# First attention of a fused transformer kernel: where TensorE computes the four heads' output product, and in which PSUM bank

## What is computed

```
q, k = rope(hs @ Wq.T), rope(hs @ Wk.T);  v = hs @ Wv.T;  g = hs @ Wg.T
s  = clip(hs @ Ws1.T @ Ws2.T + bs2, -32, 32);  z = cumlogsumexp(s, over tokens)
A  = where(mask, q @ k.T * scale, 0)
ok = exp(-z) * (A @ exp(s))                       # slot scores
qv = softmax(ok)
W2 = where(mask, (qv * exp(-z)) @ exp(s).T, 0)    # slot weights
o  = W2 @ v                                       # values
o_g = rmsnorm(o) * gnorm * silu(g)
x   = x + o_g @ Wo.T                              # output product
```

## Time and profile before

| | us |
|---|---|
| median of 3 runs (lowest, highest) | 1480.73 (1479.02, 1484.91) |
| the profiled execution's own time | 1484.12 |
| its span, first to last instruction | 1482.3 |
| PE busy, of the span | 1342.1 (91%) |
| PEld busy | 1069.0 (72%) |
| DVE busy | 921.8 (62%) |
| POOL busy | 556.5 (38%) |
| ACT busy | 517.4 (35%) |
| mean granted TensorE clock, as a share of 2.4 GHz | 0.967 |

### The profile page before, as it was taken

One profiled execution on the slowest core, in us unless ns is written; L12 is line 12 of the kernel. 1 busy time (PEld: TensorE's weight loads), 2 busy tenths in 40 slices (PEclk: granted clock), 3 DMA queues, 4 the chain that ended last, 5 costly groups with the idle time before them and its releaser, 6 DMA issues. The chain is left out here.

```text
span 1482.3 us, 47081 instructions
## 1 busy us (share of the span) xinstructions
PE 1342.1 (91%) x19926; PEld 1069.0 (72%) x19926; DVE 921.8 (62%) x1825; ACT 517.4 (35%) x1188; POOL 556.5 (38%) x608
## 2 busy tenths in 40 slices
PE   2899999999999999999986699999998688997996
PEld 2678788888788788788765577777777466776665
DVE  2777777777777777777764474242423245666886
ACT  2244444444444444444343313231322122222343
POOL 0656555556565565655532212222212111112111
PEclk9999999999999999999999799999999789997999
DMA  6000000010000100000001500000000630000620
GB/s 188 5 14 13 13 13 13 14 31 13 13 13 13 31 13 13 7 3 2 2 3 38 206 12 1 0 0 0 0 1 0 184 107 0 0 0 2 197 67 22
DMA packets 33416, 47.09 MB, mean 32 GB/s; under 512 B 6974, under 2 KB 22552, under 8 KB 32728
## 3 DMA queue, kind: packets, MB, share of 16 engines
q1 hardware_dynamic: 31048, 42.20, 9.3%
q10 hardware_dynamic: 2112, 2.10, 0.5%
q0 software_dynamic: 80, 0.26, 0.1%
HBM read 42.19 MB, written 2.36 MB: 30 GB/s over the span
## 5 line engine op out<-in xcount | busy, mean ns | idle before, releaser
L419 PE MATMUL OE<-w_o,ogT_s 128*128 128x256 f32 x512 | 137.9, 392 | 0.7 <-ACT ogT_s L506 0.7
L875 POOL TENSOR_TENSOR hT_lo<-h,hT_hi 128x512 fp32r<-128x512 f32 x44 | 56.8, 1292 | 193.1 <-ACT hT_hi L1048 193.1
L233 POOL TENSOR_TENSOR turned<-t1c,t2s 128x512 f32<-128x512 f32 x62 | 78.8, 1271 | 123.0 <-DVE t2s L636 123.0
L661 DVE RECIPROCAL enz<-SC 128x128 f32<-128x128 f32 x128 | 121.3, 949 | 2.9 <-PE SC L367 2.5
L274 POOL TENSOR_TENSOR exz<-ex,enz 128x256 f32<-128x256 f32 x64 | 47.4, 740 | 181.2 <-ACT ex L572 181.2
L1111 DVE SCALAR_TENSOR_TENSOR t<-th,m 128x512 f32<-128x512 f32 (+1 forms) x56 | 38.4, 685 | 121.3 <-ACT th L1053 93.5
L318 PE MATMUL PJ<-hs_hi,w_hi 128*128 128x512 f32 x248 | 102.6, 414 | 0.0
L329 PE MATMUL PJ<-w_hi,hs_lo 128*128 128x512 f32 x256 | 100.3, 392 | 0.5 <-issue 0.5
L329 PE MATMUL PJ<-w_hi,hs_hi 128*128 128x512 f32 x256 | 100.8, 394 | 0.0
L329 PE MATMUL PJ<-w_lo,hs_hi 128*128 128x512 f32 x256 | 100.3, 392 | 0.0
L318 PE MATMUL PJ<-hs_hi,w_lo 128*128 128x512 f32 x248 | 97.3, 392 | 0.0
(11 more groups left out here) (383 smaller groups left out, 3574.9 us busy)
## 6 DMA issues: line engine op xcount, KB each, us to landing
we_ring<-in_we SPq DMA_DIRECT2D x64, 256.0 KB, 3.1
w_raw<-in_w_slices SPq DMA_DIRECT2D x48, 128.0 KB, 2.1
turned<-in_w_slices ACTq DMA_DIRECT2D x4, 512.0 KB, 7.9
xres<-in_x SPq DMA_DIRECT2D x2, 1024.0 KB, 14.4
out_rows<-xres SPq DMA_DIRECT2D x16, 128.0 KB, 1.7
w1r<-in_w1i SPq DMA_DIRECT2D x1, 1408.0 KB, 6.6
w_s<-in_w SPq DMA_DIRECT2D x2, 682.0 KB
w_o<-in_wo SPq DMA_DIRECT2D x1, 1024.0 KB, 5.4
```

Of the source, the lines that this page charges most:

```text
L233: pool.tensor_tensor(to[:, 0, :], x1c[:, :], x2s[:, :], ALU.subtract)
L419: m = pe.matmul(OE[:, SW:SW + D], ogT_s[:, i % 2, h * P:(h + 1) * P], w_o[:, i // G % 2, h, :], start=(h == 0), stop=(h == HQ - 1))
L661: dve.reciprocal(enz[:, cols], SC[:, SW:2 * SW][:, cols]).then_inc(z_rec, 1)
L875: eng.tensor_tensor(hT[1][s, m % 2, :], h[s, m % 2, :], hT[0][s, m % 2, :].bitcast(F32), ALU.subtract).then_inc(second, 1)
```

## The change

In `heads_out` the product is summed in the lower half of `PJ[0]` in place of the upper half of `OE`, and its four heads are issued one by one: before `turn_og`, between `slot_weights` and `turn_es`, between `scores` and `values`, and between `values` and `slot_scores`. Before, it was two and two, at the first two of these places. The waits follow the bank: `heads_out` waits until `PJ[0]` has been read (`x1_sin`, `v_ev`) where it waited for `ok_z`; `proj_v` waits for `y_add`, and `slot_scores` no longer does. DVE does `mask_scores(i+1)` ahead of `y_out(i-2)`.

```diff
             def proj_v(i, part):
                 if part.start == 0:
                     pe.wait_ge(x1_sin, min(FIRST + i, TURNS))
+                    pe.wait_ge(y_add, i - 2) if i >= 3 else None
                     pe.wait_ge(v_ev, i)
@@
             def slot_scores(i):
                 pe.wait_ge(a_mask, i + 1)
                 pe.wait_ge(ok_z, i)
-                pe.wait_ge(y_add, i - 2) if i >= 3 else None
@@
                     pe.wait_ge(ogT_ev, i + 1)
                     pe.wait_ge(y_add, i)
-                    pe.wait_ge(ok_z, min(i + 3, STEPS))
+                    pe.wait_ge(x1_sin, min(i + 3 + FIRST, TURNS))
+                    pe.wait_ge(v_ev, min(i + 3, STEPS))
                     pe.wait_ge(wo_scaled, i // G + 1)
                 for h in range(*part):
-                    m = pe.matmul(OE[:, SW:SW + D], ogT_s[:, i % 2, h * P:(h + 1) * P], w_o[:, i // G % 2, h, :],
+                    m = pe.matmul(PJ[0][:, 0:D], ogT_s[:, i % 2, h * P:(h + 1) * P], w_o[:, i // G % 2, h, :],
                                   start=(h == 0), stop=(h == HQ - 1))
@@
                 if now:
                     turn_p(i)
                 if i >= 2:
-                    heads_out(i - 2, (0, 2))
+                    heads_out(i - 2, (0, 1))
                 if i >= 1:
                     turn_og(i - 1)
                 if now:
                     slot_weights(i)
                 if i >= 2:
-                    heads_out(i - 2, (2, HQ))
+                    heads_out(i - 2, (1, 2))
                 if one:
                     turn_es(i + 1)
                     scores(i + 1)
+                if i >= 2:
+                    heads_out(i - 2, (2, 3))
                 if now:
                     values(i)
+                if i >= 2:
+                    heads_out(i - 2, (3, HQ))
                 if one:
                     slot_scores(i + 1)
@@
             def y_out(i):
                 dve.wait_ge(y_mm, i + 1)
-                dve.tensor_tensor(xres[:, i % G, :], OE[:, SW:SW + D], xres[:, i % G, :], ALU.add).then_inc(y_add, 1)
+                dve.tensor_tensor(xres[:, i % G, :], PJ[0][:, 0:D], xres[:, i % G, :], ALU.add).then_inc(y_add, 1)
@@
                     z(i + 1, 1)
+                if one:
+                    mask_scores(i + 1)
                 if i >= 2:
                     y_out(i - 2)
                 if one:
-                    mask_scores(i + 1)
                     slot_max(i + 1)
```

## The result

The changed kernel takes 1516.2 us (median of 4 runs, 1512.8 to 1518.1), the kernel before 1481.1 us beside it: a ratio of 1.0223, 95% interval 1.0199 to 1.0247. The forecast was 1510, 2.0% slower, with a range of 1498 to 1523. The profiled execution has a span of 1515.3 us, 33.0 more than before.

A forecast was written before the change was run, and what follows sets the result against it. TensorE, busy 649.8 of 660 us, was taken as the bound; +30.5 us for the moved heads, +6 for `turn_es`, -9 for gaps and +1.5 for last rounds gave +29 on 1480.7, so 1510 us, range 1498 to 1523.

The forecast's parts named there:

- isolated head until small tiles: One head alone between small tiles: 0.43 us, +0.10 behind small tiles, +0.09 to 0.10 until they restart, so 0.63, twice.
- `values` until a head: Edge from `values`, now 0.86 us to `slot_scores`: with a head behind it 1.01, so +0.15.
- TensorE is a plain sum: First attention's loop: a round sums TensorE's start-to-start distances; anything else counts only where it makes TensorE wait.
- Changes of tile: TensorE switching between whole-array and small-tile work loses about 0.1 us each way; moved heads cost about +0.50 us a round.
- Rival D: Not slower: a head between small tiles costs only its 0.43 us; 1472, or 1478 with the `turn_es` wait; chance 0.07.
- Rival E: Weight loads hidden: the 0.10 us a head pays behind small tiles goes, 1498 us; chance 0.05.
- The new wait of `turn_es`: Ahead of `scores`, `turn_es` comes early and its load waits for ACT's copy to `ogT_s`: +0.1 us a round, +6 us.
- Rival C: Chain ahead of `scores` bounds: `ogT_s`, then `turn_es` and `wm` 0.2 us later a round, +12, 1522 us; chance 0.10.
- The longer rounds: Gaps, mostly inside `slot_scores`, about 10 us in all, read as waits for code; most go, -9 us.
- rival B: The gaps stay, being no code waits or packets falling due elsewhere as densely: 1519 us; chance 0.14.
- DVE and the new bank at nothing: DVE's work ahead of `scores` (`wm` 0.3 us early) and the new bank with its waits cost nothing.
- The last rounds: Four or five rounds wait for POOL's norm in `turn_og`; a moved head no longer fills it: +0.3 each, +1.5 us.

The follow-up runs named there:

- f3: Changed kernel with both late heads together behind `scores` and none behind `values`: 1500.4 us, ratio 1.0131.
- f5: Changed kernel with heads one, two, one: before `turn_og`, two behind `slot_weights`, one behind `values`, none behind `scores`: 1501.1 us, ratio 1.0134.
- f7: Changed kernel with two heads before `turn_og`, none between `slot_weights` and `turn_es`, one behind `scores`, one behind `values`: 1541.0 us, ratio 1.0396.
- f1: Changed kernel (its bank, waits and VectorE order) with the heads two and two at the two old places: 1485.9 us, ratio 1.0022.

## Why the prediction was right, point by point

| term | predicted | measured |
|---|---|---|
| isolated head until small tiles | 0.63 us, twice | 0.63, 0.63 |
| `scores` until a head | 0.69 | 0.68 |
| `values` until a head | 1.01 | 1.01 |
| late `turn_es` | +0.1 | +0.12 (0.09 and 0.03) |
| regular round | 11.95 to 12.05 | 12.01 |
| gaps | -9 us | -10 us |
| first attention | +29 us | +28.5 us |
| last rounds, over the +0.6 of each | +1.5 us | +1.6 us |
| behind it | 0 | +4.5 us in this profile, +2.3 in the second |

- *TensorE is a plain sum* held: the regular round of every variant came out within 0.1 us of what was added up for it beforehand.
- *Changes of tile* held, as a price for each place (f3) and with the dearer edge behind `values` (f5). Rival D is out: the extra in a round is 0.60, far above 0.16. Rival E is out too: the load of an isolated head starts with its matmul, and the distance of 0.63 has the 0.10 in it.
- *The new wait of `turn_es`* held in size (0.12 against 0.1), and f5 and f7 show it go and grow. Two errors in its working cancel, and that is luck. It had the hand-over at 0.06, taken from DVE's `ok`; from the copy `ogT_s` to the matmul it is 0.14. The late load was put at 0.10 and showed as 0.03. The sign named for it, ScalarE's `ogT_s` in the waits, did not come: the view says "issue". Rival C, a chain ahead of `scores` that is 0.2 us later still, is out: `turn_es` pays 0.12, and `wm` is done 0.34 before `scores`.
- *The longer rounds* went, and the list's shift with the count of the gaps shows why: rival B, by which they would stay, is out. I had bounded the relief by nothing and 10 us and taken 9. What I held against B, that all gaps lie in one line, was misread: three of the 11 lie in other lines. What I held for B, that their place hangs on the position in the list, is true, but from it does not follow that they stay.
- *DVE and the new bank at nothing* held (f1).
- *The last rounds* held. Four of the last five wait for POOL's norm, and that wait grew from 0.58 to 0.60 us each to 1.02 or 1.03, as forecast. The five, from one `turn_p` to the next, take 52.03 us before (from 742.64) and 56.70 now (from 765.23), +4.67; less 0.6 for each round, 1.6 to 1.7 are left.

```profile
777.44 0.63 PE L372 MATMUL TB<-ident,og 128*128 128x128 f32 x4 [1.03 <-POOL og L241]
```

- *What was off:* the total, +35 us on the median against +29. 4.5 us are the blocks behind, for which I gave no term at all. Another 1.5 come from the executions that happened to be profiled: the one before took 3.0 us more than the median beside the changed kernel, the changed one 1.6 more than its own. Why the blocks behind take longer is open in part: more gaps in the second attention and a lower clock are seen, their cause is not. The total of 1516 lies between the forecast and rival B's 1519 and could not have told them apart; the gaps that went do.

No version here beats the kernel before. Its order pays for the fewest changes of tile, and its 10 us of gaps cost less than one more place does (0.17 + 0.12 us a round in f3, some 17 us, with its gaps nearly gone).

## What to carry to other kernels

In this kernel, whole-array work put between two lots of small tiles paid 0.2 us for each place, the same for one head as for two, plus 0.15 between `values` and `slot_scores`, which are tiles of one kind; so before spreading filler, look in the timeline whether the place has idle time to fill. When TensorE is the bound, add start-to-start distances instead of trusting its busy share, which rose here while the kernel got slower. Before an accumulator moves later, look who writes its bank next: the same spread cost 37 us more in the old bank. Where TensorE goes through 256 instructions in some 2 us, look for waits for code.

## What I had not expected

- Waits for code that lengthen a round of an unrolled loop by up to 1.4 us, all at one place of a block of 256 instructions. Two kernels compared in one round can differ by such a gap, and it means nothing.
- The hand-over from ACT's `ogT_s` or DVE's add to a waiting matmul took 0.14 to 0.15 us in three kernels (0.11 to its load), that from TensorE to DVE 0.06. It is no fixed figure for the pair of engines: from ACT's `v_s` to the load that waits for it, it was 0.05 (426.12 + 0.58 against 426.75). Why they differ is open.
- The blocks behind, the same program text, took between 670.4 us (list shifted, clock 0.94) and 680.3 us (changed kernel, clock 0.92), each counted from about 3 us ahead of the second block's first matmul.

```profile
807.30:1477.70 670.40, 584.26 (x6847) 450.16 (x6846) 346.79 (x657) 187.82 (x351) 127.69 (x163) 0.94 0.15 46
```
